# The experts' down projection of a mixture layer: two full 32-bit matmuls replaced by five in a rounded format

## The reference

```python
xn = layernorm(x)
# branch 1: K, V, Q from layernorm(xn) with gamma, beta; K and V are turned by a rotary table
A = sum over the tokens of K/|K| * V/|V|;  A = 0.5*A + 0.5
branch1 = (A * Q) @ W_out + b_out + xn
# branch 2: 16 experts of width 176, 4 per token, at most 128 tokens for each expert
xg  = xn[tokens of expert e]                          # 128 x 256
mid = silu(xg @ w_gate[e]) * (xg @ w_up[e])           # 128 x 176
y[tokens of expert e] += (mid @ w_down[e]) * weight   # 128 x 256
branch2 = y + (silu(xn @ sw_gate) * (xn @ sw_up)) @ sw_down    # shared expert, width 352
out = x + branch1 + branch2
```

## Time and profile before

| | us |
|---|---|
| median of 3 runs | 194.8 |
| lowest, highest | 194.12, 194.98 |
| the profiled execution | 194.25 |
| its span, first to last instruction | 192.4 |
| PE busy | 172.1 |
| POOL busy | 107.2 |
| DVE busy | 109.0 |
| ACT busy | 76.8 |
| mean granted clock of TensorE | 0.935 of full |

### The profile page before, as it was taken

How to read it: one execution, slowest core, us unless ns; L and a number is a source line. 1 busy time by engine, 2 the same in 40 slices (tenths; PEclk the granted TensorE clock), 3 DMA queues, 4 the chain that set the end, 5 groups by cost and what they waited for, 6 DMA issues and landing times.

```text
span 192.4 us, 3141 instructions
## 1 busy us (share of the span) xinstructions
PE 172.1 (89%) x1029; PEld 141.8 (74%) x1029; DVE 109.0 (57%) x304; ACT 76.8 (40%) x230; POOL 107.2 (56%) x125
## 2 busy tenths in 40 slices
PE   6953999699987798999999997999999999999970
PEld 4733858599976667888777785876788788689970
DVE  2364216996797733555497839273585542355490
ACT  3031005268856868744545652254332242430000
POOL 4309800889850062469876888858737633330870
PEclk9995558979999999999999999799999999999998
DMA  6997957031106672177476544734557322215957
GB/s 170 344 376 246 480 185 255 3 109 68 45 0 141 161 238 73 23 174 161 136 172 172 145 144 67 174 102 91 151 123 175 73 30 27 27 11 156 296 176 264
DMA packets 25363, 28.68 MB, mean 149 GB/s; under 512 B 4098, under 2 KB 24163, under 8 KB 25316
## 3 DMA queue, kind: packets, MB, share of 16 engines
q1 hardware_dynamic: 20898, 23.04, 38.5%
q0 software_dynamic: 3072, 4.33, 13.2%
q10 hardware_dynamic: 1378, 1.12, 1.8%
HBM read 21.79 MB, written 8.79 MB: 159 GB/s over the span
## 4 chain that ended last, share of the span: by engine, by line
PE 62%; DVE 12%; POOL 9%; issue 7%; DMA 7%; ACT 1%; DVEq 0%; POOLq 0%
PE bank L233 12%; PE bank L234 10%; PE bank L235 10%; PE bank L1058 7%; DMA ysum<-eo,idx 5%; PE bank L1069 4%; PE bank L890 3%; PE bank L1068 3%; PE bank L924 2%; PE bank L1094 2%; POOL ysum L382 2%; PE bank L894 2%; PE bank L900 2%; POOL wtok L391 1%; POOL xg L374 1%
## 5 line engine op out<-in xcount | busy, mean ns | idle before, releaser
L382 POOL DMA_INDIRECT ysum<-eo,idx x16 | 25.8, 1610 | 19.6 <-DMA ysum<-eo,idx 9.1
L374 POOL DMA_INDIRECT xg<-rows,idx x16 | 20.8, 1298 | 25.9 <-issue 14.8
L233 PE MATMUL bank<-wkvr_s,xt_all 128*128 128x256 f32 (+1 forms) x96 | 30.5, 318 | 3.5 <-DVE xt_all L644 1.7
L234 PE MATMUL bank<-wkvr_s,xt_all 128*128 128x256 f32 (+1 forms) x96 | 28.5, 296 | 0.0
L235 PE MATMUL bank<-wkvr_s,xt_all 128*128 128x256 f32 (+1 forms) x96 | 28.4, 296 | 0.0
L1058 PE MATMUL bank<-xgt,wgu 128*128 128x128 f32 (+1 forms) x192 | 24.0, 275 | 0.0
L233 PEld LDWEIGHTS bank<-wkvr_s,xt_all 128*128 128x128 f32 x96 | 19.4, 202 | 5.3 <-DVE xt_all L644 2.3
L1058 PEld LDWEIGHTS bank<-xgt,wgu 128*128 128x128 f32 (+1 forms) x192 | 22.3, 187 | 0.0
L233 PE MATMUL bank<-xt_all,sw_s 128*128 128x512 f32 (+1 forms) x48 | 20.7, 432 | 0.0
L234 PE MATMUL bank<-xt_all,sw_s 128*128 128x512 f32 (+1 forms) x48 | 19.5, 406 | 0.0
L235 PE MATMUL bank<-xt_all,sw_s 128*128 128x512 f32 (+1 forms) x48 | 19.4, 404 | 0.0
(11 more groups left out here) (158 smaller groups left out, 380.1 us busy)
## 6 DMA issues: line engine op xcount, KB each, us to landing
wgu<-in_w_gu SPq DMA_DIRECT2D x16, 368.0 KB, 3.1
rows<-xn_all SPq DMA_DIRECT2D x4, 512.0 KB, 3.2
wdn<-in_w_dn SPq DMA_DIRECT2D x16, 128.0 KB, 3.1
x_all<-ysum SPq DMA_DIRECT2D x4, 512.0 KB, 7.1
x_all<-in_x SPq DMA_DIRECT2D x3, 512.0 KB, 7.2
trg<-in_trig SPq DMA_DIRECT2D x1, 1024.0 KB, 10.3
out<-xn_all ACTq DMA_DIRECT2D x4, 256.0 KB, 2.2
out<-xn_all SPq DMA_DIRECT2D x4, 256.0 KB, 2.6
```

The source lines that it names most:

```text
L233: nc.tensor.matmul(dst, lt_hi, r_hi, start=start, stop=False)
L234: nc.tensor.matmul(dst, lt_hi, r_lo, start=False, stop=False)
L374: nc.gpsimd.indirect_dma_start(out=xg[:, e % G, :], out_offset=None, in_=rows, in_offset=bass.IndirectOffsetOnAxis(ap=idx[:, e:e + 1], axi ...
L382: nc.gpsimd.indirect_dma_start(out=ysum, out_offset=bass.IndirectOffsetOnAxis(ap=idx[:, e:e + 1], axis=0), in_=eo[:, e % G, :], in_offset= ...
```

## The change

The down projection of each expert is computed as the shared expert's already is, from a rounded part and a rest of both operands. `mid` is copied by ACT to a rounded `mid_h` (`middle_hi`), and DVE subtracts to get the rest (`middle_lo`). The weights `wdn` are copied by ACT to a rounded part (`down_hi`), and POOL subtracts to get the rest (`down_lo`). For features 0 to 127 PE does the three matmuls of `mm3`. For features 128 to 175 the 48 rows of the rest lie at partitions 64 to 111 of the same tile as the rounded part, and the weights' last 48 rows are loaded twice, at partitions 0 and 64; one matmul over 112 partitions then makes hi x hi and lo x hi, and a second over 48 makes hi x lo. `sil` and `mid` become one tile, `wdn` has two buffers instead of four, and some small tiles share memory. The unused partitions are set to zero once. The diff, cut to what matters:

```diff
-        wgu, wdn = sb("wgu", [P, G, DC, GU]), sb("wdn", [P, G, 2, D])
+        bout_row = minus_bet[0:1, :, :].rearrange("p c n -> p (c n)")
+        wgu, wdn = sb("wgu", [P, G, DC, GU]), sb("wdn", [P, 2, 2, D])
+        junk_k = diag[:, :, :].rearrange("p b e -> p (b e)").bitcast(BF16).rearrange("p (k n) -> p k n", k=2)
+        sil = mid
+        mid_h, mid_l, wdn_s = sb("mid_h", [P, 2, 2, P], F32R), sb("mid_l", [P, 2, P], F32R), sb("wdn_s", [P, 2, 2, 2, D], F32R)
...
 # SP
-            def load_expert(e):
-                j = e % G
-                sp.dma_start(wgu[:, j, :, :], w_gu[e, :, :].rearrange("(c p) n -> p c n", p=P)).then_inc(ew_in[j], 16)
-                sp.dma_start(wdn[:, j, 0, :], w_dn[e, 0:P, :]).then_inc(ew_in[j], 16)
-                sp.dma_start(wdn[0:I2, j, 1, :], w_dn[e, P:I, :]).then_inc(ew_in[j], 16)
+            def load_down(e):
+                if e >= 2:
+                    sp.wait_ge(wd_lo, e - 1)
+                sp.dma_start(wdn[:, e % 2, 0, :], w_dn[e, 0:P, :]).then_inc(dn_in[e % 2], 16)
+                for row in (0, UP2):
+                    sp.dma_start(wdn[row:row + I2, e % 2, 1, :], w_dn[e, P:I, :]).then_inc(dn_in[e % 2], 16)
+            def load_gate_up(e):
+                sp.dma_start(wgu[:, e % G, :, :], w_gu[e, :, :].rearrange("(c p) n -> p c n", p=P)).then_inc(gu_in[e % G], 16)
...
+            sp.wait_ge(sv_done, 4)
+            sp.dma_start(bout_row, b_out).then_inc(mix_in, 16)
...
+            sp.wait_ge(mid_zero, 2)
+            for e in range(2):
+                load_gate_up(e)
+                load_down(e)
...
+            load_gate_up(2)
+            load_gate_up(3)
+            load_down(2)
             for e in range(G, E):
                 sp.wait_ge(gu_done, e - G + 1)
-                sp.wait_ge(d_done, e - G + 1)
-                load_expert(e)
+                load_gate_up(e)
+                load_down(e - 1)
+            load_down(E - 1)
...
 # POOL
             pool.memset(acc[:, :, :], 0.0).then_inc(zero_set, 1)
+            pool.memset(mid[:, :, :, :], 0.0).then_inc(mid_zero, 1)
...
             spread_of(2)
+            pool.memset(wdn[:, :, 1, :], 0.0).then_inc(mid_zero, 1)
...
+            def down_lo(e):
+                pool.wait_ge(wd_hi, e + 1)
+                nc.gpsimd.tensor_tensor(wdn_s[:, e % 2, 1, :, :], wdn[:, e % 2, :, :], f(wdn_s[:, e % 2, 0, :, :]), ALU.subtract).then_inc(wd_lo, 1)
...
                 if e + 3 < E:
                     gather(e + 3)
-                if e:
+                if e == 0:
+                    down_lo(0)
+                else:
                     scatter(e - 1)
+                if e + 1 < E:
+                    down_lo(e + 1)
                 for i in KEYS[e]:
                     rotate(i)
...
 # ACT
             def silu(e):
                 k = e % 2
                 if e >= 2:
-                    act.wait_ge(mid_done, 2 * (e - 1))
+                    act.wait_ge(mid_lo, 2 * (e - 1))
+                else:
+                    act.wait_ge(mid_zero, 1)
...
+            def middle_hi(e):
+                k = e % 2
+                if e >= 2:
+                    act.wait_ge(d_done, e - 1)
+                act.wait_ge(mid_done, 2 * e + 2)
+                nc.scalar.activation(mid_h[:, k, :, :], mid[:, k, :, :], ACT.Copy).then_inc(mid_hi, 1)
+            def down_hi(e):
+                act.wait_ge(dn_in[e % 2], 48 * (e // 2 + 1))
+                if e >= 2:
+                    act.wait_ge(d_done, e - 1)
+                    act.wait_ge(wd_lo, e - 1)
+                nc.scalar.activation(wdn_s[:, e % 2, 0, :, :], wdn[:, e % 2, :, :], ACT.Copy).then_inc(wd_hi, 1)
...
                 silu(e)
                 if q is not None:
                     shared_hi(q)
+                middle_hi(e)
                 if e:
                     weigh(e - 1)
+                else:
+                    down_hi(0)
+                if e + 1 < E:
+                    down_hi(e + 1)
...
 # DVE
             def gated(e):
                 k = e % 2
-                if e >= 2:
-                    dve.wait_ge(d_done, e - 1)
                 dve.wait_ge(silu_done, 2 * e + 2)
...
+            def middle_lo(e):
+                k = e % 2
+                dve.wait_ge(mid_hi, e + 1)
+                nc.vector.tensor_tensor(mid_l[:, k, :], mid[:, k, 0, :], f(mid_h[:, k, 0, :]), ALU.subtract).then_inc(mid_lo, 1)
+                nc.vector.tensor_tensor(mid_h[UP2:UP2 + I2, k, 1, :], mid[0:I2, k, 1, :], f(mid_h[0:I2, k, 1, :]), ALU.subtract).then_inc(mid_lo, 1)
...
                 if q is not None:
                     shared_lo(q)
+                middle_lo(e)
                 for i in KEYS[e]:
                     products(i)
...
 # PE
             def down(e):
-                j, k = e % G, e % 2
-                pe.wait_ge(mid_done, 2 * e + 2)
+                k = e % 2
+                pe.wait_ge(mid_lo, 2 * e + 2)
+                pe.wait_ge(wd_lo, e + 1)
...
-                nc.tensor.matmul(bank[5][:, 0:D], mid[:, k, 0, :], wdn[:, j, 0, :], start=True, stop=False)
-                nc.tensor.matmul(bank[5][:, 0:D], mid[0:I2, k, 1, :], wdn[0:I2, j, 1, :], start=False, stop=True).then_inc(d_done, 1)
+                both = UP2 + I2
+                mm3(bank[5][:, 0:D], mid_h[:, k, 0, :], mid_l[:, k, :], wdn_s[:, k, 0, 0, :], wdn_s[:, k, 1, 0, :], True, False)
+                nc.tensor.matmul(bank[5][:, 0:D], mid_h[0:both, k, 1, :], wdn_s[0:both, k, 0, 1, :], start=False, stop=False)
+                nc.tensor.matmul(bank[5][:, 0:D], mid_h[0:I2, k, 1, :], wdn_s[0:I2, k, 1, 1, :], start=False, stop=True).then_inc(d_done, 1)
```

More of the change, by code:

```diff
@@ L106, in layer @@
         gam, bet = gb_cols[:, 0:DC], gb_cols[:, DC:2 * DC]
-        bout_row = sb("bout_row", [1, D])
         one_col, expo = sb("one_col", [P, 1]), sb("expo", [P, G, 2])
@@ L128, in layer @@
         nrm, wprod, wtok = sb("nrm", [P, TILES, 2]), sb("wprod", [P, TILES]), sb("wtok", [P, TILES])
-        junk = sb("junk", [P, 4, D], BF16)
+        junk_v = sb("junk", [P, 2, D], BF16)
         acc = sb("acc", [P, BATCH, 2 * D])
@@ L147, in layer @@
         xg, eo = sb("xg", [P, G, ROW]), sb("eo", [P, G, D])
-        xgt, sil, mid = sb("xgt", [P, 2, DC, P]), sb("sil", [P, 2, 2, P]), sb("mid", [P, 2, 2, P])
+        xgt, mid = sb("xgt", [P, 2, DC, P]), sb("mid", [P, 2, 2, P])
+        sil = mid
+        mid_h, mid_l, wdn_s = sb("mid_h", [P, 2, 2, P], F32R), sb("mid_l", [P, 2, P], F32R), sb("wdn_s", [P, 2, 2, 2, D], F32R)
         smid_s = sb("smid_s", [P, 3, 2, G * P], F32R)
@@ L185, in layer @@
             sem(n) for n in ("zero_set", "ones_set", "table_set", "pads_saved", "ysum_set", "xn_saved", "wd_saved"))
-        ew_in, gath = sems("ew_in", G), sems("gath", G)
+        gu_in, dn_in, gath = sems("gu_in", G), sems("dn_in", 2), sems("gath", G)
         bn_done, ag_done, ve_done, rr_done, vv_done, v2_done, v2_pool, pow_done, first_done, norm_done = (
@@ L191, in layer @@
         swf_done, sw_hi, sw_lo = sem("swf_done"), sem("sw_hi"), sem("sw_lo")
+        mid_zero, mid_hi, mid_lo, wd_hi, wd_lo = (sem(n) for n in ("mid_zero", "mid_hi", "mid_lo", "wd_hi", "wd_lo"))
         t_done, hi_done, lo_done, vr_done, v_kept, k_done, k_kept = (
@@ L277, in _ @@
             sp.dma_start(wo[:, :, :], w_out.rearrange("(c p) n -> p c n", p=P)).then_inc(mix_in, 16)
-            sp.dma_start(bout_row[:, :], b_out).then_inc(mix_in, 16)
+            sp.wait_ge(sv_done, 4)
+            sp.dma_start(bout_row, b_out).then_inc(mix_in, 16)
             save_xn(2)
@@ L480, in square @@
                 if keys:
-                    nc.scalar.activation(junk[:, t % 2, :], k_all[:, t, :], ACT.Square, accum_out=nrm[:, t, 0:1]).then_inc(ksq_done, 1)
+                    if t == 0:
+                        act.wait_ge(tb_chain, 2)
+                    nc.scalar.activation(junk_k[:, t % 2, :], k_all[:, t, :], ACT.Square, accum_out=nrm[:, t, 0:1]).then_inc(ksq_done, 1)
                 else:
-                    nc.scalar.activation(junk[:, 2 + t % 2, :], vr_all[:, t, 0:D], ACT.Square, accum_out=nrm[:, t, 1:2]).then_inc(vsq_done, 1)
+                    nc.scalar.activation(junk_v[:, t % 2, :], vr_all[:, t, 0:D], ACT.Square, accum_out=nrm[:, t, 1:2]).then_inc(vsq_done, 1)
             hi_one(0)
@@ L1051, in gate_up @@
                 j, k = e % G, e % 2
-                pe.wait_ge(ew_in[j], 48 * (e // G + 1))
+                pe.wait_ge(gu_in[j], 16 * (e // G + 1))
                 if e >= 2:
```

4 lines of the change are left out of this document (removed).

## The result

The changed kernel takes 200.4 us (median of four runs, 198.8 to 201.5), the kernel before 194.9 beside it (four runs, 194.1 to 198.5): ratio 1.029, 95% interval 1.019 to 1.039. It is slower by 5.5 us; forecast was slower by 3.2. The profiled executions lie further apart than the medians: 201.46 with a span of 199.6, against 194.25 with 192.4, so the traces have 7.2 us to account for.

A forecast was written before the change was run, and what follows sets the result against it. POOL's queue was taken to bound the first half of the expert stage, PE leading behind it. Second reduction +4.5, three down projections -1.3: +3.2 on 194.8 gives 198.0, range 190 to 203.

The forecast's parts named there:

- third rival: Expert stage: POOL's subtractions and DVE's two-input steps collide (3.6 more) and the low clock returns: +8, 203; chance 0.10.
- What PE gains: Down projection on PE: five rounded matmuls take 0.95 for 1.37, saving 0.42 per expert, 6.7 for 16.
- POOL's first half: POOL up to rotation 7: six subtractions, 7.7, of which 4.6 shows, plus a start 1.2 late: 5.8 late.
- second rival: Half covered: start only 0.4 late, some DVE-POOL collisions fall away, reduction lags 2 to 4: 192 to 196; chance 0.15.
- The first reduction: Token reduction at iteration 8: 5.8 late behind POOL's rotations, from 117.36 to 123.2, with PE idle.
- The second reduction: Behind rotations 14 and 15: they end 6.5 late at 158.9, accumulations need 1.4, so 160.3: +4.5.
- The three downs behind it: Three down projections on PE after the second token reduction, together saving 1.3.
- The clock: PE's clock behind its wait at the reductions: the earlier stretch at 0.87 lost about 1.7 in 13 us.
- POOL's collisions: POOL and DVE steps reading SBUF hold each other up, by about 0.6 per meeting.
- Lost whole, or not: First eight experts: POOL sets the first reduction, so PE's 3.4 (8 x 0.42) becomes idle time and is lost.
- ACT's `down_hi`: ACT's weight copy behind `weigh`: expected to wait once, for expert 2, delaying `silu` by nothing to 2; taken as nothing.
- signs of being wrong: Reduction at or before 117, no PE idle time there, or `down_lo` showing waits of its own on ACT's copy.

The follow-up runs named there:

- fills: Changed kernel with POOL's subtraction replaced by two fills of the same 128x512, which read nothing, the weights' rest zero: 193.7 on repeat (195.4 first), ratio 0.985.
- The experiment with POOL's wait: Changed kernel with POOL in iteration 13 waiting for all accumulations before `down_lo`: 195.5, ratio 1.004.
- two columns: Changed kernel with POOL subtracting only 2 of each expert's 512 weight columns, the rest otherwise zero: 190.1, ratio 0.974.
- the subtraction on DVE: Changed kernel with the weights' subtraction moved from POOL to DVE, behind the iteration's products, same values: 192.6, ratio 0.991.

## Why the prediction was right, and where it was not

It was right in its direction and its range, and in that POOL's subtraction and not PE decides. Of the mechanism it had the smaller part. Its sum is made of queue time, and with fills in the queue, which hold it nearly as long, the kernel is faster than the one before (0.985, where the sum says 198). What cost most are the meetings with DVE and the clock behind them, which the forecast put into its third rival at a chance of 0.10. That the sum came near is in good part luck. Step by step:

- **What PE gains** was mis-sized: 0.42 forecast. Iterations with 512 columns went from 5.60 to 5.32 and those of the kept piece from 4.95 to 4.68: 0.27 to 0.28. The five come as forecast (0.20, 0.12, 0.12), but the fifth 0.09 late, the unit behind 0.19 late and its second matmul another 0.10. The step that failed is the reading of the earlier trace rows: the 0.62 behind the old narrow matmul was taken for the price of full 32 bits. Part of it was the price of 48 rows, and the new order pays that too.
- **POOL's first half**: 1.27 per subtraction as forecast, but the end of the rotations moved by 3.25 and not by 5.8. The scatter of 82.11 came 1.56 late (1.2 forecast), and from there on only 1.7 of 7.6 shows. Hidden were nearly all of the two transfer waits (3.1), 0.9 of the wait before the gather, and 1.8 in one small product for the token weights that took 2.57 before and 0.79 after. Before, it ended with DVE's run of products and accumulation (91.9). The forecast had hidden 3.1. That meetings fall away or shrink when two engines are shifted against each other stood in the second rival.
- **The first reduction**: 121.85, forecast 123.2. From the rotations' end it took 2.65 in place of the 1.41 that the forecast carried over: the two parts of `middle_lo` (118.65, 119.39) stand ahead of the products and were still running. The forecast let them "come late with it" and gave that no number. DVE had itself waited 2.31 for ACT's silu at 117.50, and that for PE's gate and up, which ran at the low clock (its group took 2.32 for 1.49); how much of the delay is the clock's is not separated. Nor is PE idle for several us just ahead of the reduction: its wait there is 0.22, and the idle time stands at 111.47, 2.78 long, behind the `shared_lo` of 109.41 that POOL held up.
- **The second reduction**: 160.42, forecast 160.3, by two errors that cancel. The rotations end at 155.93 and not at 158.9, and behind them stand 4.5 and not 1.4, since the accumulations meet `down_lo`. The experiment with POOL's wait shows this share. The 6.5 by which the forecast had the rotations late stands there without its steps; it was 3.5.
- **The three downs behind it** bring 0.5 for the 1.3 forecast.
- **The clock** was left out of the sum and is what is missing: 2.9 to 3.1 in the trace behind the second reduction. The forecast had PE idle for several us ahead of a reduction and a lower clock behind the like wait, and put the two together only in the third rival. It priced multiplied meetings and the low clock at +8; both came, and the traces lie 7.2 apart, the medians 5.5.
- **POOL's collisions**, about 0.6 each in the forecast from the earlier trace rows, cost 1.3 to 2.3 each (2.00 for 0.69, 3.87 for 1.53). At 153.80 DVE was held not by one instruction but by a run of them (subtraction, then the rotations).
- **Lost whole, or not**: the forecast says that PE's gain in the first eight experts is lost, since POOL sets that point. Widening the kernel before's matmul, which leaves POOL's work alone, moved the first reduction by 2.8. The step that failed is the reading of POOL's queue as a fixed schedule: its waits and the length of its small products depend on when PE and DVE reach them, and in that run most of the 2.8 came from there.
- ACT's `down_hi` did not hold up the silu, as forecast; the tail is moved and not changed, as forecast. Of the signs of being wrong, `down_lo` did wait for ACT's copy, but once, at the very start.

Shown by runs: the subtraction costs by what it reads more than by its time in the queue (two columns; fills); one meeting and what follows it are worth 4.9 by the medians and 6.5 by the traces; PE's slot does not set the time of the changed kernel. Open: how the rest of the loss divides among the meetings of the first half. No experiment held POOL off DVE there alone.

## What to carry to other kernels

Before a rest is computed on POOL, list DVE's steps with two inputs in SBUF and who waits for them: the price is that of the meetings and of the idle PE behind them. A subtraction of the same size cost some 2 to 3 us in one kernel and 10 in another. Look at a narrow matmul between full ones first: padding it to full height with zero rows gained 4% here, while five rounded matmuls in the place of the pair brought at most about the same. A forecast that makes PE wait should price the lower clock behind it: it came with each wait of 2.5 to 3.2 in the traces here, and with some of 1.2 to 2.2 (1.16 in the kernel before, 1.90 in the first trace of the fills) but not with others (1.41 in the second, 1.81 with the subtraction on DVE).

## What the runs showed of the hardware

A matmul of 48 rows between full ones shows no overlap of its weight load with the matmul before it, and neither does the full one behind it. PE's weight loads in the kernel before, with the narrow matmul and the unit behind it:

```profile
145.61 0.29 PEld L1069 LDWEIGHTS bank<-wdn,mid 48*128 48x128 f32 x2 [0.33 <-issue]
146.24 0.19 PEld L233 LDWEIGHTS bank<-swd_s,smid_s 128*128 128x128 f32 x1 [0.33 <-issue]
146.35 0.19 PEld L234 LDWEIGHTS bank<-swd_s,smid_s 128*128 128x128 f32 x1
```

And the same place with the matmul over 128 rows:

```profile
93.40 0.30 PEld L1073 LDWEIGHTS bank<-wdn,mid 128*128 128x128 f32 x2
93.73 0.41 PEld L1074 LDWEIGHTS bank<-wdn,mid 128*128 128x128 f32 x2
94.16 0.19 PEld L233 LDWEIGHTS bank<-xt_all,sw_s 128*128 128x128 f32 x1
```

With 48 rows each load starts with its matmul (145.61 and 145.62; 146.24 and 146.24) behind a gap of 0.33; with 128 it starts while the matmul before still runs (93.73, its matmul at 93.94). The changed kernel shows the same at 95.81 (matmul 95.82) and 96.13, and not at its pieces of 96 and 112 rows. From the start of the down projection to the second matmul of a shared piece of 512 columns:

| | 48 rows | widened |
|---|---|---|
| full 32 bits | 1.48 | 1.10 |
| rounded and rest | 1.29 | 0.92 |

Both forms lose 0.37 to 0.38 by it, twice what separates the forms.

That a matmul of few rows costs PE more than one of all 128 was no part of the forecast. What the chip does between the two loads is not shown; that the loss goes with the height of the tile is (112 for 48 rows, and 128 for 48).
